# Tail of a transformer block kernel: the feed-forward output steps in two row tiles of 64, gate products over two pairs of banks, one store issued ahead of the softmax reciprocals

## What is computed

```
x = x + alpha1(t) * attention(ada_rmsnorm(x, t))          # 16 heads of 16
n = ada_rmsnorm(x, t)                                     # gamma(t) * rmsnorm(x) + beta(t)
x = x + alpha2(t) * (silu(n @ gate.T) * (n @ hidden.T) @ out_w.T + out_b)   # hidden width 1024
x = layernorm(x) * w + b + tanh(t @ lin_w.T + lin_b);  out = x * w + b
```

## Time and profile before

| | |
|---|---|
| median of three runs | 748.59 us (746.62 to 749.01) |
| the profiled execution | 748.02 us, span 746.2 us |
| instructions | 17410 |
| TensorE busy | 708.5 us (95%) |
| VectorE busy | 532.1 us (71%) |
| ScalarE busy | 467.2 us (63%) |
| GpSimd busy | 392.2 us (53%) |
| granted TensorE clock | 0.987 of full |

### The profile page before, as it was taken

How to read it: one execution, slowest core, us unless ns; L and a number is a source line. 1 busy time by engine, 2 the same in 40 slices (tenths; PEclk the granted TensorE clock), 3 DMA queues, 4 the chain that set the end, 5 groups by cost and what they waited for, 6 DMA issues and landing times.

```text
span 746.2 us, 17410 instructions
## 1 busy us (share of the span) xinstructions
PE 708.5 (95%) x6660; PEld 498.4 (67%) x6660; DVE 532.1 (71%) x797; ACT 467.2 (63%) x860; POOL 392.2 (53%) x493
## 2 busy tenths in 40 slices
PE   6698999899999999999999999999999999999995
PEld 5343444567777667776777667767777667679895
DVE  4787787777677876877677867778677776336765
ACT  4467777765667666776666766676667665753431
POOL 4364242543368544865367543876267454872533
PEclk9889999999999999999999999999999999999998
DMA  8677657345443645274453654255353620332210
GB/s 230 171 240 243 201 165 276 111 158 189 161 131 118 202 153 157 66 217 143 144 163 116 208 163 158 61 187 151 110 183 96 212 82 7 89 90 65 57 45 29
DMA packets 63275, 107.17 MB, mean 144 GB/s; under 512 B 10480, under 2 KB 18344, under 8 KB 63192
## 3 DMA queue, kind: packets, MB, share of 16 engines
q1 hardware_dynamic: 61892, 104.66, 45.3%
q10 hardware_dynamic: 1172, 1.20, 0.6%
q0 software_dynamic: 128, 0.20, 0.1%
HBM read 57.50 MB, written 37.52 MB: 127 GB/s over the span
## 4 chain that ended last, share of the span: by engine, by line
PE 78%; DVE 7%; ACT 5%; DMA 3%; issue 3%; POOL 2%; SPq 1%; ACTq 0%; POOLq 0%; DVEq 0%
PE ps_x L1484 19%; PE ps_o L1460 13%; PE ps_o L1497 12%; PE ps_j L1355 11%; PE ps_s L1444 8%; PE ps_m L1425 6%; DVE mx L1175 3%; ACT prob L968 2%; PE ps_m L1484 2%; PE ps_s L1484 1%; PE ps_j L1393 1%; DMA n_x<-n 1%; PE ps_j L1361 1%; DMA qs<-m_hl 1%; DMA d_c<-reciprocal_scratch 1%
## 5 line engine op out<-in xcount | busy, mean ns | idle before, releaser
L1175 DVE TENSOR_REDUCE mx<-ps_m 128x2 f32<-128x1024 f32 x211 | 256.8, 1217 | 62.1 <-PE ps_m L1425 61.8
L968 ACT ACTIVATE prob<-ps_s 128x1024 f32<-128x1024 f32 x219 | 223.6, 1021 | 46.4 <-PE ps_s L1444 44.5
L1460 PE MATMUL ps_o<-prob,v 128*32 128x512 f32 x1024 | 127.5, 600 | 0.1
L1444 PE MATMUL ps_s<-qs,ks 64*128 64x512 f32 x438 | 101.5, 458 | 8.3 <-issue 3.7
L675 POOL TENSOR_TENSOR a_lo<-act_y,a_hi 128x256 fp32r<-128x256 f32 x100 | 73.7, 737 | 54.5 <-ACT a_hi L1001 54.4
L1484 PE MATMUL ps_x<-n,gh_hi 64*128 64x256 f32 x872 | 99.1, 285 | 0.2 <-DVE act_y L1218 0.2
L1484 PE MATMUL ps_x<-n_x,gh_hi 64*128 64x256 f32 x872 | 97.1, 280 | 0.6 <-DMA n_x<-n 0.6
L1425 PE MATMUL ps_m<-ks,qs 64*128 64x512 f32 x422 | 89.0, 416 | 4.7 <-ACT prob L968 1.8
L1444 PEld LDWEIGHTS ps_s<-qs,ks 64*128 64x128 f32 x438 | 41.6, 185 | 77.3 <-issue 54.5
L1216 DVE SCALAR_TENSOR_TENSOR act_y<-act_y,ps_x 128x256 f32<-128x256 f32 x109 | 45.6, 418 | 61.3 <-ACT act_y L994 61.3
L1484 PEld LDWEIGHTS ps_x<-n,gh_hi 64*128 64x128 f32 x872 | 75.4, 186 | 9.1 <-DVE act_y L1218 6.4
(11 more groups left out here) (182 smaller groups left out, 1489.6 us busy)
## 6 DMA issues: line engine op xcount, KB each, us to landing
qs<-stack_scratch SPq DMA_DIRECT2D x30, 512.0 KB, 4.6
ks<-stack_scratch SPq DMA_DIRECT2D x30, 512.0 KB, 6.2
stack_scratch<-qk_hi SPq DMA_DIRECT2D x56, 256.0 KB, 3.4
out_scratch<-o_raw SPq DMA_DIRECT2D x32, 256.0 KB, 2.3
n_x<-n SPq DMA_DIRECT2D x32, 256.0 KB, 3.6
stack_scratch<-qk_lo SPq DMA_DIRECT2D x28, 256.0 KB, 3.8
on_lo<-out_scratch SPq DMA_DIRECT2D x16, 256.0 KB
d_c<-reciprocal_scratch SPq DMA_DIRECT2D x16, 256.0 KB
```

What stands on the lines that cost most here:

```text
L968: act.activation(prob[:, n % 3, 2 * h:2 * h + 2, :], score_pair(n, h)[:], ACT.Exp, scale=SCALE).then_inc(p_r, 1)
L1175: dve.tensor_reduce(mx[:, group % 2, :, h, qt], max_pair(mp)[:], AX.X, ALU.max).then_inc(mx_red, 1)
L1444: mm = pe.matmul(score_pair(n, j)[:, s, :], ks[r:r + 64, g, j, kb * P:(kb + 1) * P], qs[r:r + 64, g, j, :], start=True, stop=True)
L1460: mm = pe.matmul(ps_o[32 * i:32 * i + 32, :], v[:, at:at + 32], prob[:, n % 3, i, :], start=(kb == 0), stop=(kb == TT - 1), skip_group_che ...
```

## The change

Nothing before unit 128 is altered. In the tail:

- The output steps O(96) to O(127) are 12 matmuls of 64 rows instead of 6 of 128. The row tile r = 0 sums into the first bank of `ps_s`, r = 1 into the second.
- The gate products of the tail take `ps_m` and `ps_x` in turn, and no longer `ps_s`.
- `scale` of a half's end takes three VectorE instructions: a copy of the first bank, the second bank added, the product with the table. The next half's first O waits for the second of them.
- O(96) waits for the last exponentials (`p_r`) and not for the copy of `ps_o`.
- In units 130 and 146 SyncE issues the store of the older half and the table load one unit earlier, in unit 130 that is ahead of `rec_write` and `rec_read`.

```
-            return ps_x if e < TAIL else (ps_m, ps_x, ps_s)[(e - TAIL) % 3]
+            return ps_x if e < TAIL else (ps_m, ps_x)[(e - TAIL) % 2]
...
+                if at(2, -3) and n >= NU:
+                    store(b - 3, 1)
+                if at(2, -2) and n >= NU:
+                    load_tab_b(b - 2)
                 if at(3, -1) and b > 1:
                     rec_write(b - 1, 1)
...
-                if at(3, -3):
+                if at(3, -3) and n < NU:
                     store(b - 3, 1)
-                if at(3, -2):
+                if at(3, -2) and n < NU:
                     load_tab_b(b - 2)
...
-                    dve.tensor_tensor(sc[:], ps_f, tab_f[:].unsqueeze(1).broadcast_to([P, 2, D]),
-                                      ALU.mult).then_inc(sc_r, 1)
+                    factor = tab_f[:].unsqueeze(1).broadcast_to([P, 2, D])
+                    if what[0] == "F":
+                        dve.tensor_tensor(sc[:], ps_f, factor, ALU.mult).then_inc(sc_r, 1)
+                    else:
+                        top, bottom = (ps_s[:, r].rearrange("p (t n) -> p t n", t=2) for r in range(2))
+                        halves = what[1] - CHUNKS * CH // JC
+                        dve.tensor_copy(sc[:], top).then_inc(f_sum_r, 1)
+                        dve.wait_ge(f_sum_r, 2 * halves + 1)
+                        dve.tensor_tensor(sc[:], bottom, sc[:], ALU.add).then_inc(f_sum_r, 1)
+                        dve.wait_ge(f_sum_r, 2 * halves + 2)
+                        dve.tensor_tensor(sc[:], sc[:], factor, ALU.mult).then_inc(sc_r, 1)
...
                 if j == 0:
                     if CH * CHUNKS == e:
-                        pe.wait_ge(o_r, NG * B)
+                        pe.wait_ge(p_r, 2 * NU)
                     else:
-                        pe.wait_ge(sc_r, SC_NO["H", hf - 1])
-                project_out(e, ps_f, j == 0, j == JC - 1)
+                        pe.wait_ge(f_sum_r, 2 * (hf - CHUNKS * CH // JC))
+                a_made(e)
+                for t in range(2):
+                    for m, (a, c) in enumerate(PARTS):
+                        for r in range(2):
+                            rows = slice(64 * r, 64 * r + 64)
+                            mm = pe.matmul(ps_s[:, r, D * t:D * t + D], A[a][rows, e % RING, t * P:(t + 1) * P],
+                                           OW[c][rows, j, :], start=(j == 0 and m == 0 and t == 0),
+                                           stop=(j == JC - 1 and m == 2), skip_group_check=True)
+                mm.then_inc(f_done, 1)
```

More of the change, by code:

```diff
@@ L226, in build @@
         gh_full = sem("gh_full"); t_r = sem("t_r"); s_r = sem("s_r"); y_r = sem("y_r")
-        a_hi_r = sem("a_hi_r"); a_lo_r = sem("a_lo_r"); a_tail_r = sem("a_tail_r"); f_done = sem("f_done")
+        a_hi_r = sem("a_hi_r"); a_lo_r = sem("a_lo_r"); a_tail_r = sem("a_tail_r"); f_done = sem("f_done"); f_sum_r = sem("f_sum_r")
         stat_r = sem("stat_r"); mv_r = sem("mv_r"); centre_r = sem("centre_r"); rstd3_r = sem("rstd3_r")
@@ L1486, in gate_hidden, with a_made @@
                 mm.then_inc(gh_full, 1)
-            def project_out(e, out, first, end):
-                j = e % JC
+            def a_made(e):
                 if e < TAIL:
@@ L1494, in project_out @@
                     pe.wait_ge(a_tail_r, e - TAIL + 1)
+            def project_out(e, out, first, end):
+                j = e % JC
+                a_made(e)
                 for t in range(2):
```

## The result

| | before | with the change |
|---|---|---|
| median | 746.91 us (746.53 to 749.01, 5 runs) | 752.75 us (752.56 to 753.27, 5 runs) |
| profiled execution, its span | 748.02, 746.2 us | 753.27, 751.4 us |
| instructions | 17410 | 17802 |
| TensorE, VectorE busy | 708.5, 532.1 us | 707.5, 537.5 us |
| ScalarE, GpSimd busy | 467.2, 392.2 us | 466.6, 391.6 us |

The ratio is 1.0065, with a 95% interval of 1.0046 to 1.0084: the change makes the kernel slower by 0.65%. I had forecast "within 0.3%" at 749.8 us, with 0.16 for slower; the measured time lies above my range, which ended at 751.9 us.

The account below looks back on a forecast made before the run. TensorE was taken to bound the kernel, with 78% of the chain; 0.75 + 1.05 - 1.8 + 1.4 = +1.4 us gave 749.4 us against the profiled 748.02 us, 750.0 us on the median, given as 749.8 us; range 746.9 to 751.9 us.

Parts of the forecast that it names:

- Step 1: Tail up to WO0: TensorE ready 1.5 us earlier, only about 0.6 us of it usable; two pairs of banks enough.
- Step 2: Reciprocals' DMAs before WO0: store and load ahead make the write land 0.85 us later, WO0 start 0.3 us later.
- rival C: Reciprocals' write held up as in the worst row, 4.37 us: delay 1.96 us, sum +2.5 us, 751.1 us; chance 0.13.
- Step 3: WO0 to FT0: four tile changes instead of two and four output steps, +0.45 us; FT0 0.75 us later in all.
- Step 4: End of half 13: O(112) waits for copy and addition, 0.7 us later; output steps after it 1.05 us later.
- Step 5: Steady tail to the end of G(126): ten tile changes between gate and output steps go, -1.8 us.
- rival D: Tail: the 0.2 us are the price of another operand or bank, not tile; sum +3.0 us, 751.6 us; chance 0.04.
- Step 6: Behind the last output step: copy and addition lie bare on the chain, +1.4 us.

Follow-up runs that it names:

- e5: The kernel before with its tail's gate products over two pairs of banks, nothing else: 747.75 against 748.29 us, ratio 0.9994.
- e2: The kernel before with only SyncE's order changed, store and table load ahead of the reciprocals' write: 748.41 against 747.99 us, ratio 0.9988.
- f1: The changed kernel measured again, unaltered, beside the kernel before: 752.07 against 747.67 us, ratio 1.0058.
- e3: The changed kernel with 22 extra matmuls, results thrown away, just before WO0: 751.41 us against 747.99 us for the kernel before, ratio 1.0043.
- e1: The changed kernel with SyncE's earlier order, reciprocals first, then store and table load: 750.3 us against 747.99 us for the kernel before, ratio 1.003.
- e6: e1 with 72 already satisfied waits at the head of TensorE's program: 750.32 us against 748.29 us for the kernel before, ratio 1.0036.
- e4: The changed kernel with one VectorE instruction for three at a half's end, second bank's sums left out: 749.89 against 747.99 us before, ratio 1.0031.
- e8: The kernel before with 36 already satisfied waits ahead of TensorE's work: 750.4 against 748.29 us, ratio 1.0024.
- f3: f2 with VectorE's scale of half 13 one gate step later: 747.18 us against 747.67 us for the kernel before, ratio 0.9993.
- f2: The kernel before with row tiles in half 14 only, the same kernel as m14 measured again: 746.72 against 747.67 us, ratio 0.9985.
- f4: m14 with half 12 in tiles too, two bank pairs throughout and 72 satisfied waits: 746.35 us against 747.67 us for the kernel before, ratio 0.9977.
- m14: The kernel before with row tiles in half 14 only: 746.95 against 748.29 us, ratio 0.9991.

## Why the prediction was wrong

**Step 1, TensorE up to WO0: right.** TensorE was ready early and did not bind. Two pairs of banks were enough (e5).

**Step 2, the reciprocals' DMAs: the mechanism right, its size wrong.** This is the first failure. I took +0.85 us for the write between bounds of 0 and 1.96, by the bytes at the rate of a full stretch. It measured +1.79 us (4.20 against 2.41), almost the upper bound, and in e2 alone +1.78. The amount of data was right and the rate was wrong. I had put 671 KB at 201 GB/s, 3.34 us. In the change the stretch that begins as far ahead of the write's issue (672.64 us) moves 682 KB up to 676.80 us, but at 164 GB/s and with the engines busy only 0.58: 4.16 us, and the last 0.56 us to the landing are nearly empty, as the last 0.43 us were before. So the step "it is the nearer of the two ends because the DMA engines were busy only 0.40" failed too: free engines did not help a 16 KB write behind 384 KB that were issued in the 1.2 us ahead of it. The nearest row was the earlier trace rows, 4.37 us behind 768 KB, and I should have taken it. So rival C's mechanism held (it decides from 4.1 us), with 0.13 in my list. The rule of the Trainium skill (DMA: Bandwidth & Descriptors, section on queues, rings and completion order), that each DMA engine consumes descriptors in ring order, agrees with the trace: 4.19 to 4.35 us with the data ahead, 2.31 to 2.71 us without. Whether the write waits its turn behind these bytes or only shares the engines with them, no run here separates.

I missed 0.72 us more in the same step: the store of `o_raw`, which the change doesn't touch, took 2.74 us, because the fetch of instructions met it. Together, from the rows: +0.72 store, -0.04 from its read to the write's issue, +1.79 write, -0.13 read, -0.24 GpSimd and ScalarE, -0.46 slack (0.61 us before, 0.15 now) gives the +1.64 us. The gain of up to 0.65 us in the read behind the write, which I had left out, is not there: 4.20 against 4.33 us.

**Step 3, WO0 to FT0: a mechanism was missing.** This is the second failure, as large as the first in time and the graver one, since a whole term was missing. I had written that TensorE would stand idle for 1.7 us, and put the cost of that at nothing. It stood idle for 3.03 us, and the granted clock fell to 0.50 as WO0 began (in f1, 0.7 us behind its first matmul). With TensorE kept busy (e3) the stretch takes 9.28 us, without 10.79: 1.5 us for the clock. So the cost of a wait in front of TensorE is here not only its length. The tile changes of this stretch, which I had put at 0.45 us, cost 0.25 to 0.28 us at the full clock (e1, e3, e6); where the 0.2 us are saved I did not look into.

The two failures hang together. Behind the write of 2.63 us (e1) the idle time is 1.93 us, and the clock stays. Behind the write of 4.20 us and the late store it is 2.96 to 3.44 us in three kernels (the change, f1, e4), and it falls in all three. With my 0.85 us the idle time might have stayed short of that. But the length of one hole does not decide it alone. The same level came, for 3.4 us each time, behind holes of 1.81 us (e3, which ended at 185.67 us; the clock fell at 187.2) and 2.14 us (e8, above), and in before at 150.7 us with no hole over 0.7 us in the five us ahead (the row of before, in the form of the rows above):

```profile
151.00:154.00 3.00, 3.00 (x26) 2.44 (x24) 1.27 (x2) 0.74 (x3) 1.17 (x2) 0.50 0.02 5
```

In the two us ahead of that TensorE had two holes, of 0.68 and 0.51 us. What decides between the two levels is not shown by these runs.

**Step 4, the end of half 13: right.** +0.77 for +0.7 us to O(112), +0.43 for +0.35 us to O(114). By e4 it is the copy and the addition: without them -0.72 and -0.69 us. The copy measured 687 ns, near my 0.66 us. VectorE's groups from 700 us on show it beside the addition (busy us, mean ns, idle before):

```profile
L1199 DVE TENSOR_TENSOR sc<-ps_s,sc 128x512 f32<-128x512 f32 x3 | 2.1, 691 | 0.1
L1201 DVE TENSOR_TENSOR sc<-sc,tab_f 128x512 f32<-128x512 f32 x3 | 2.1, 691 | 0.1
L1197 DVE COPY sc<-ps_s 128x512 f32<-128x512 f32 x3 | 2.1, 687 | 1.1 <-PE ps_s L1537 1.1
```

The Trainium skill (VectorE: DVE Perf Modes, on why PSUM operands drop a tier) has a float32 instruction with a PSUM operand at the single rate, and here the trace agrees: 687 ns for the copy, 691 ns for the additions.

**Step 5, the steady tail: right.** -1.82 us for -1.8. 0.19 to 0.20 us is the price of a change of tile and not of other operands (rival D): without changes two steps of each kind take 4.30 us. The Trainium skill says in a sentence that changing the mode drains TensorE (TensorEngine Tiling (Array Packing), Key Properties); here the trace agrees that a change costs something, 0.19 to 0.20 us each.

**Step 6, the end: right in its mechanism, 0.35 us short.** +1.75 for +1.4 us. e4 puts 1.4 us on the copy and the addition. The other 0.3 us is the last low part, 0.73 us where it was 0.44, and it is there in e4 too (0.81 us), so it is not the copy's. In the change GpSimd's product `xr` (740.12 to 741.40 us) runs beside it, where before it had ended 0.1 us ahead of it; that this is the cause was not tried by itself.

In sum, of the 3.8 us that I was short on the span (5.2 for 1.4), 1.3 us are the write and the store up to WO0, 1.3 us are the stretch behind it, 0.5 us small misses in steps 4 and 6, and 0.7 us are the part ahead of `o_raw`, where the kernels are the same and which moves by more than that between executions.

**Still open:** which engine's code is fetched where, and so how an edit moves it (e6 moved it far away, e8 by a few tenths of a us); whether before would lose 0.7 to 1.0 us in a collision (e8 did not make one); what decides when the granted clock falls; and what makes the part ahead of `o_raw` vary by 5 us. The clock may be a part of that: the three executions that start `o_raw` latest (e8 at 670.9, e3 at 669.1, f3 at 667.9 us) all have a stretch of 3.4 us at 0.50 in their first 200 us besides the start's, but before, e1 and e2 have one too and start it at 666.2 to 666.7 us.

## What to carry to other kernels

A small DMA on which the critical path waits is priced here by what was issued just ahead of it on the same queue, not by the average load of the DMA engines: a store without a due date belongs behind it. A wait that leaves TensorE idle can cost more than its length, since the clock may be at half when the work comes; fill the hole, or keep it short, though a short hole is no guarantee. And row tiles that remove changes of tile pay only where the second bank's sum is hidden: in a middle half they bring over 1 us (f2, 1.35 us), in the last one the sum lies bare and takes it back.

## What the runs showed that I had not expected

- **The granted clock fell after a hole of 3 us in a busy stretch**: 2.96, 3.03 and 3.44 us of idle time ahead of WO0 were followed by the 0.50 level for some 3 us (f1, the change, e4), and 0.72, 1.39, 1.48 and 1.93 us by none (e2, f4, e6, e1). Elsewhere 1.81 and 2.14 us were enough (e3, e8), and once two holes of under 0.7 us (before), so no limit can be read from this. Matmuls of 256 columns then start 0.21 us apart instead of 0.12. It costs 1.5 us here.
- **Fetching the program uses the DMA engines that the data use.** One packet of 16 KB on one engine for about 1 us, met by a 256 KB store, makes that store 2.7 to 3.2 us instead of 2.0 (shown by moving it in e1 and e6; the change, e3, e4 and f1 have it in the same place). In before, e2, e5, m14, f2 and f3 it came just behind the data. So an edit elsewhere in the program can lengthen a DMA far away from it, here by up to 1.2 us, and a single execution of a changed program holds such differences that have nothing to do with the edit's purpose.
- **A write of 16 KB took 1.43, 2.4 or 4.2 us** with nothing, 256 KB, or 256 KB and another 384 KB ahead of it (e2).
